# q placed by transfers, context loads four units ahead, ternary weights and expert loads moved, in a two-pass cross-attention kernel

## The reference

```
def bit_quant(W):
    gamma = jnp.mean(jnp.abs(W))
    Wq = jnp.clip(jnp.round(W / (gamma + Q_EPS)), -1.0, 1.0) * gamma
    return W + jax.lax.stop_gradient(Wq - W)
...
q = xn @ bit_quant(Wq).T + bq
k = context @ bit_quant(Wk).T + bk
v = context @ bit_quant(Wv).T + bv
scores = jnp.einsum('bqhd,bkhd->bhqk', q, k) * SCALE
probs = jax.nn.softmax(scores, axis=-1)
out = jnp.einsum('bhqk,bkhd->bqhd', probs, v).reshape(B, T, C)
return residual + (out @ bit_quant(Wo).T + bo)
```

## Time and profile before

| | |
|---|---|
| median of 3 runs | 638.69 us (638.66 to 639.59) |
| the profiled execution | 638.79 us, its span 637.0 us |
| mean granted clock of TensorE | 0.935 of full |
| TensorE busy | 544.5 us (85% of the span) |
| VectorE busy | 425.6 us (67%) |
| ScalarE busy | 326.7 us (51%) |
| GpSimd busy | 152.7 us (24%) |
| windows of the first pass | 106 to 327 us |
| windows of the second pass | 431 to 627 us |

### The profile page before, as it was taken

How to read it: one execution, slowest core, us unless ns; L and a number is a source line. 1 busy time by engine, 2 the same in 40 slices (tenths; PEclk the granted TensorE clock), 3 DMA queues, 4 the chain that set the end, 5 groups by cost and what they waited for, 6 DMA issues and landing times.

```text
span 637.0 us, 16158 instructions
## 1 busy us (share of the span) xinstructions
PE 544.5 (85%) x6582; PEld 383.9 (60%) x6582; DVE 425.6 (67%) x1090; ACT 326.7 (51%) x495; POOL 152.7 (24%) x128
## 2 busy tenths in 40 slices
PE   0699838589999999999967989468999999999996
PEld 0587515266766667676745767234666767667674
DVE  5667478679998999977224302569787687786730
ACT  0165214356666576765743333215566567676573
POOL 1554212313241524300015100223041240421000
PEclk9899668889999999999997989878999999999998
DMA  5010733434436353342200642026536436353300
GB/s 154 32 50 1 164 92 69 126 88 110 132 74 172 72 139 75 75 99 50 100 1 1 170 108 66 9 84 146 137 80 175 121 77 168 88 137 75 74 3 15
DMA packets 25338, 57.44 MB, mean 90 GB/s; under 512 B 4660, under 2 KB 8876, under 8 KB 25268
## 3 DMA queue, kind: packets, MB, share of 16 engines
q1 hardware_dynamic: 25268, 56.45, 34.6%
HBM read 17.81 MB, written 0.23 MB: 28 GB/s over the span
## 4 chain that ended last, share of the span: by engine, by line
PE 45%; DVE 23%; issue 21%; DMA 4%; POOL 3%; ACT 2%; SPq 2%; DVEq 0%; POOLq 0%; ACTq 0%
DVE mxp L791 11%; PE SM L1170 10%; PE PO L1185 9%; PE ST L1149 6%; PE MI L1101 6%; DMA cx<-in_ctx 3%; PE MI L1091 3%; DVE cx L779 3%; DVE qst L815 2%; PE MI L1125 2%; PE SM L1257 2%; DVE ksplit L786 1%; DVE cstat L763 1%; PE SM L1125 1%; DVE xn L732 1%
## 5 line engine op out<-in xcount | busy, mean ns | idle before, releaser
L791 DVE TENSOR_REDUCE mxp<-SM 112x1 f32<-112x500 f32 x364 | 235.2, 673 | 60.5 <-PE SM L1170 59.1
L593 ACT ACTIVATE PT<-ST 128x896 f32<-128x896 f32 x192 | 171.1, 911 | 49.7 <-PE ST L1149 49.1
L1170 PE MATMUL SM<-kst,qst 96*112 96x500 bf16 x364 | 143.1, 407 | 24.7 <-DVE mxp L791 24.1
L1149 PEld LDWEIGHTS ST<-qst,kst 98*128 98x128 bf16 x1536 | 95.0, 100 | 32.6 <-issue 9.7
L1149 PE MATMUL ST<-qst,kst 98*128 98x112 bf16 x1536 | 108.5, 215 | 1.2 <-DMA qst<-mrow 1.2
L471 POOL TENSOR_TENSOR kr<-kf,ksplit 128x500 f32<-128x500 f32 x48 | 56.1, 1170 | 184.4 <-ACT ksplit L565 184.3
L1185 PE MATMUL PO<-PT,vaug 125*32 125x112 f32 x3072 | 96.5, 264 | 2.1 <-ACT PT L593 1.5
L1170 PEld LDWEIGHTS SM<-kst,qst 96*112 96x112 bf16 x364 | 46.8, 131 | 66.9 <-DVE mxp L791 55.2
L1185 PEld LDWEIGHTS PO<-PT,vaug 125*32 125x32 f32 x3072 | 70.5, 110 | 24.5 <-issue 14.9
L577 ACT ACTIVATE vaug<-MI 125x512 f32<-125x512 f32 x48 | 28.7, 598 | 79.4 <-PE MI L1101 79.4
L476 POOL TENSOR_TENSOR ksplit<-kr,ksplit 128x500 bf16<-128x500 f32 x48 | 54.5, 1135 | 53.4 <-DVE ksplit L786 53.4
(11 more groups left out here) (129 smaller groups left out, 555.4 us busy)
## 6 DMA issues: line engine op xcount, KB each, us to landing
kst<-ksplit SPq DMA_DIRECT2D x192, 187.5 KB, 3.8
cx<-in_ctx SPq DMA_DIRECT2D x8, 750.0 KB
xT<-in_ctxT SPq DMA_DIRECT2D x8, 750.0 KB, 4.6
moe<-in_w1T SPq DMA_DIRECT2D x8, 256.0 KB, 2.9
moe<-in_w2T SPq DMA_DIRECT2D x8, 256.0 KB, 3.3
qall<-qsplit SPq DMA_DIRECT2D x12, 112.0 KB, 2.3
watt<-in_watt SPq DMA_DIRECT2D x1, 768.0 KB, 5.8
qst<-mrow SPq DMA_DIRECT2D x32, 1.8 KB
```

What stands on the lines that cost most here:

```text
L593: nc.scalar.activation(PT[:, k % PTB], ST[:, k % 2, :, 0:4 * PC], ACT.Exp, scale=SCALE).then_inc(exp_done, 1)
L791: nc.vector.tensor_reduce(mxp[:, j // 3, j % 3:j % 3 + 1], tile_bank(j, banks), AX.X, ALU.max).then_inc(sm_red, 1)
L1149: last = mm(ST[:, k % 2, cc, PC * p:PC * (p + 1)], kst[n.par][:, 4 * half + p, at:at + 128], qst[n.par][:, 4 * half + p], start=True, stop ...
L1170: mm(tile_bank(j, banks), qst[n.par][0:SROWS, j // 3], kst[n.par][0:SROWS, j // 3, at:at + THIRD], start=True, stop=True).then_inc(sm_full, 1)
```

## The change

1. `place_q` stays for the first unit of each pass. For all others a new function `place` on SyncE copies q into `qst` by two transfers per half (one per head of the pair), each 48 rows by 4 pairs by 56 elements of bf16. The zeros come from a memset of GpSimd at the start. TensorE waits for the transfers by a new function `q_here`.
2. In the first pass `load_ctx` is issued for n+4 where it was for n+3; the load of u3 moves to behind `load_qall(0)`.
3. The ternary weights move from behind `split_q(0)` into the window of u5, behind the maxima of step 6.
4. The loads of the first two experts move to the ends of SyncE's windows 3 and 4.

```
+            def place(n, half):
+                if n.c == 1:
+                    sp.wait_ge(qall_loaded, 16 * TERMS * (n.s + 1))
+                if n.s or n.c >= 2:
+                    sp.wait_ge(st_full, (n + -2).count(STEPS, HSTEP * (half + 1)))
+                pairs = slice(4 * half, 4 * half + 4)
+                for hh in range(2):
+                    rows_of = slice(hh * DH * TERMS, (hh + 1) * DH * TERMS)
+                    sp.dma_start(qst[n.par][rows_of, pairs, L * hh:L * (hh + 1)],
+                                 qall[rows_of, pairs, L * n.c:L * (n.c + 1)]).then_inc(q_placed[half][n.par], 16)
...
             def window(n):
-                if n.s == 0 and (n + 3).exists():
-                    load_ctx(n + 3)
+                if n.s == 0 and (n + 4).exists():
+                    load_ctx(n + 4)
                 if (n + 1).exists():
+                    place(n + 1, 1)
                     restack(n + 1, 1)
                 shift(n, 1)
                 if (n + 2).exists():
+                    place(n + 2, 0)
                     restack(n + 2, 0)
                 if (n + 1).exists():
                     shift(n + 1, 0)
                 if n.s == 1 and (n + 3).exists():
                     load_xT(n + 3)
+                if n.s == 0 and n.c in (3, 4):
+                    load_expert(n.c - 3, n.c - 3)
...
-            load_expert(0, 0)
-            load_expert(1, 1)
             load_qall(0)
+            load_ctx(Unit(0, None, 3))
             shift(u0, 0)
+            place(u1, 0)
             restack(u1, 0)
             run_windows(0, window)
...
             shift(v0, 0)
+            place(v0 + 1, 0)
             restack(v0 + 1, 0)
...
             for s in range(2):
+                nc.gpsimd.memset(qst[s][0:SROWS], 0.0)
                 last = nc.gpsimd.memset(kst[s][0:SROWS, :, T:TPAD], 0.0)
...
-                        if k == Q2_STEP:
-                            place_q(nxt, 1)
-                        if k == Q1_STEP and k_unit.exists():
-                            place_q(k_unit, 0)
...
+                    if n.s == 0 and n.c == B - 3 and k == HSTEP:
+                        ternary_weights()
...
-                    if j == START_TILES - 2:
-                        place_q(first + 1, 0)
...
+            def q_here(n, half):
+                if n.c == 0:
+                    pe.wait_ge(qst_ready, 2 * n.s + half + 1)
+                else:
+                    pe.wait_ge(q_placed[half][n.par], 32 * (n.s * (3 + n.par) + n.c // 2 + n.par))
```

More of the change, by code:

```diff
@@ L303, in build_kernel @@
             sem("mparts_ready"), sem("mx_full"), sem("mx_evac"))
+        q_placed = [[sem(f"q_placed{h}{p}") for p in range(2)] for h in range(2)]
         shift_loaded = [[sem(f"shift_loaded{h}{p}") for p in range(2)] for h in range(2)]
@@ L810, in place_q @@
                     dve.wait_ge(ld_member, 32)
-                if n.s or n.it is not None or n.c >= 2:
+                if n.s:
                     dve.wait_ge(st_full, (n + -2).count(STEPS, HSTEP * (half + 1)))
@@ L836, in add_projection, with ternary_weights @@
                                         ).then_inc(x_added, 1)
+            def ternary_weights():
+                dve.wait_ge(gam_ready, 1)
+                nc.vector.tensor_scalar(thr[:, 0], gam[:], EPS, 0.5, ALU.add, ALU.mult)
+                nc.vector.tensor_scalar(thr[:, 1], gam[:], EPS, -0.5, ALU.add, ALU.mult).then_inc(thr_ready, 1)
+                dve.wait_ge(thr_ready, 1)
+                for w in range(4):
+                    nc.vector.tensor_scalar(wt[:, 0, w], watt[:, 2, w], thr[:, 0, w:w + 1], None, ALU.is_gt)
+                    last = nc.vector.tensor_scalar(wt[:, 1, w], watt[:, 2, w], thr[:, 1, w:w + 1], None, ALU.is_lt)
+                last.then_inc(tern1, 1)
+                dve.wait_ge(tern1, 1)
+                nc.vector.tensor_tensor(wt[:, 0], wt[:, 0], wt[:, 1], ALU.subtract).then_inc(tern2, 1)
+                dve.wait_ge(tern2, 1)
+                for w in range(4):
+                    last = nc.vector.scalar_tensor_tensor(out=wt[:, 1, w], in0=wt[:, 0, w], scalar=gam[:, w:w + 1],
+                                                          in1=watt[:, 2, w], op0=ALU.mult, op1=ALU.subtract)
+                last.then_inc(tern3, 1)
+                dve.wait_ge(tern3, 1)
+                nc.vector.tensor_tensor(watt[:, 2], watt[:, 2], wt[:, 1], ALU.add).then_inc(wq_ready, 1)
             def window(n):
@@ L932, in _ @@
             split_q(0)
[L935 to L951, removed]
             def start_pass(s):
@@ L1158, in scores @@
                     output_forth(n + -1)
+            def q_here(n, half):
[3 more added lines that the diff above has]
+                    pe.wait_ge(q_placed[half][n.par], 32 * (n.s * (3 + n.par) + n.c // 2 + n.par))
             def max_tile(n, j, banks=2):
                 if j == 0:
-                    pe.wait_ge(qst_ready, n.count(2, 1))
+                    q_here(n, 0)
                     pe.wait_ge(kst_loaded[0][n.par], n.par_count(16 * TERMS, 16 * TERMS))
                 if j == TILES // 2:
-                    pe.wait_ge(qst_ready, n.count(2, 2))
+                    q_here(n, 1)
                     pe.wait_ge(kst_loaded[1][n.par], n.par_count(16 * TERMS, 16 * TERMS))
```

## The result

The changed kernel took 635.05 us (median of 19 runs, 630.94 to 639.86), the kernel before 641.01 in the runs beside it (19 runs, 638.25 to 645.78): a ratio of 0.992 [0.990, 0.994]. That is 6.0 us less by the medians and 5.2 by the ratio. The profiled execution took 634.5 us, its span 632.6, against 638.8 and 637.0. The forecast was 631, with a range of 625 to 637; the measured time lies inside the range.

The account below looks back on a forecast made before the run. TensorE and VectorE were both taken as nearly full in first-pass windows, TensorE alone in the second. The terms summed to -7.6 us from 638.8, giving 631 us, range 625 to 637.

Parts of the forecast that it names:

- The stall of u0's window: u0's window: u3's context load issued earlier ends TensorE's idling and low clock, -8.8 us, 0.9 taken back for the queue: -7.9.
- The setup: Start of first pass: ternary weights out gives 0.55 us, two placement issues delay u1's keys; between -0.5 and +1.0, taken +0.3.
- VectorE's placements: Windows of u1 to u4: sparing VectorE its placements gives 0.8 us each, bounds nothing to 1.4; -3.2 us in all.
- The price of small runs: Placement transfers: 384 runs of 112 bytes per half at 48 ns each, 1.15 us per half, ahead of the keys.
- u5's window: Ternary weights hold VectorE and delay step 8's tile +4.2 us; lower clock behind the gap +2.5; spared placements -0.5.
- The second pass: Windows of v1 to v6: placements off VectorE give 0.5 us each, bounds 0 and 0.75; -3.0 us in all.
- v0: Second pass's first unit: keys issued 1.3 us later, behind placements, so v1's first tile comes later; +0.7 us.
- VectorE's time is worth something: Denies the rival that VectorE's time is worth nothing in full windows: 638.6 us, no change, chance 0.10.
- The windows don't give all they hold: Denies the rival that windows gain their full bounds, 1.4 us and 0.75 each: at best 626 us, chance 0.10.
- The clock did fall in u5's window: Denies the rival that the clock does not fall in u5's window: 628.5 us, chance 0.17.
- The stall did move into the queue: Rival: load ahead of keys and maxima row costs 2 us in u0's window, 1 in each of u1 to u3; 635, chance 0.14.
- The slower rival: Placement transfers: 112-byte runs cost three times 48 ns, delaying keys in four windows, +9.2 us; about 642, chance 0.09.

Follow-up runs that it names:

- e3: The changed kernel with the context load three units ahead again, as before the change; 640.48 us, ratio 0.999 to the kernel before.
- e4: The kernel before with only the context loads moved four units ahead; 633.12 us, ratio 0.989.
- e2: The changed kernel with q placed by VectorE again as before, all else as changed; 638.65 us, ratio 0.997 to the kernel before.
- e6: The changed kernel with the ternary weights moved into u7's window; 627.47 us, ratio 0.982 to the kernel before.
- e8: The changed kernel with each placement's runs cut into four of 28 bytes; 634.4 us, ratio 0.990 to the kernel before.
- e5: The changed kernel with the n+4 context load issued behind the second-half placement, keys and maxima row; 632.04 us, ratio 0.988 to the kernel before.
- e7: The changed kernel with ternary weights in u7's window, context load behind keys and maxima row, each pass's first placement ahead of the maxima row; 627.94 us, ratio 0.981.
- e9: The kernel of e7 with the second pass's xT load issued ahead of the next unit's maxima row; 625.75 us, ratio 0.974 to the kernel before.
- e1: The changed kernel with the ternary weights back behind split_q(0) in the setup; 628.64 us, ratio 0.980 to the kernel before.

## Why the prediction was right, and where it was off

**The stall of u0's window** (-7.9): from u1's first tile to step 6 it was 19.40 us and is 11.46, which is -7.9, and e3 and e4 show that the load's distance alone makes it. The same places, in us behind the first score of u0's window:

| kernel | q placed by | u1's first tile | step 6 | step 3 of u1 |
|---|---|---|---|---|
| before | VectorE | 7.40 | 26.80 | 50.62 |
| e4 | VectorE | 6.43 | 18.69 | 42.53 |
| e2 | VectorE | 6.64 | 18.68 | 42.37 |
| change | transfers | 7.91 | 19.37 | 42.43 |
| e6, e8 | transfers | 7.95, 7.85 | 19.14, 19.33 | 42.17, 42.36 |
| e5 (load behind) | transfers | 7.94 | 18.68 | 41.75 |
| e7, e9 (also placed early) | transfers | 6.67, 6.60 | 18.16, 19.63 | 41.23, 42.72 |

Of the 2 us that late transfers might have cost there, e5 finds about 0.5 at step 6. In e1 and e8 TensorE waits 0.3 and 0.45 us for the maxima row there. The prediction worked out from the Trainium skill that the whole 2 us would be paid; the traces show a quarter of it. e9, with the same code as e7 in this pass, is 1.5 us slower at step 3; its clock was at the lower level twice in this window, as in the change's profile, in e7 once. One sign failed: the prediction named "a clock of 1.00 there", and behind u1's first tile the clock is at its lower level for 3.41 us in the change and in every other kernel with the early load. In e4 no wait of TensorE ahead of it was longer than 1.1 us. Before the change it was 10.2 us, so the larger part came back. Of the other signs, L815 (now L835) has its 8 instructions and the windows of the second pass are near 25.0; those of u1 to u3 are not near 27.2, for which see below.

**The setup** (+0.3): the keys came 0.9 later, the tile 0.1; e1 confirms that the ternary weights had been hidden there but for 0.6 us. The first column of the table shows the price of the two issues ahead of the keys more plainly: 1.3 us, taken back by the early placement of e7. TensorE waits 1.36 us for those keys in the change's profile and 2.4 to 2.5 in e1, e5, e6 and e8. The setup itself takes up to 2.6 us more or less between executions of the same code, so that the agreement of the first stretch within 0.7 us is luck in part: e8 ends it at 149.80, the change at 148.08.

**VectorE's placements** (-3.2 for u1 to u4): the size was right, e5's four windows are 3.65 us shorter than before, 0.9 each where 0.8 was taken. The step that failed is "0 to 1.1 us late in the windows of u1 to u3; I take 0": the lateness was 1.07, 0.52 and 0.52. The estimate of when the keys would land was right; the lower bound was the wrong end to pick. In e4 the bound of 0 did hold, with no placements ahead of the keys. The rule on engines in the Trainium skill (DMA: Bandwidth & Descriptors, Why a DMA increments its semaphore by 16 and not by 1) speaks for the upper bound: by it a load of 125 rows runs on the five lowest-numbered engines. The landings agree as far as they go (6.4 us behind the load, 1.9 without), but no row names the engines, so that the load and the transfers behind it share them stays a reading. That the load's place in the order makes the loss is shown by e5. In e9 a load delays the maxima row behind it in the same way.

**The price of small runs** (1.15 us per half) was four times too high; it entered only v0's term and the lateness above, so little came of it. The Trainium skill (the same page, Specifications) says that below 512 bytes an engine reads, modifies and writes. Whether that adds to the price of a run, no run here can tell: e8 made the same packets as the change. The prediction's sum for four times the row's price also has a slip: 3.45 us more per half in four windows give 645, not 644, which changes nothing.

**u5's window** (+4.2 and +2.5, less 0.5): the gap was 4.12, the low clock lasted 3.4 us, which costs 1.7, at the lower end of the range (1.75); the block in all costs 5.5. In all four other kernels with the block there (e2, e3, e5, e8) the gap was 4.12 too, but the low clock lasted twice as long, 3.4 us lost, and the window took 29.0 to 29.7. So 2.5 lies between the two; only one of five executions lost as little as 1.7, and that the change's profile is that one is luck. The clock didn't fall there in any kernel without the block (before, e1, e4, e6, e7, e9).

**The second pass** (-3.0 for v1 to v6): 0.62 in each of the four full windows, as e2 shows, 0.35 in v5's and nothing in v6's; the late load of `xT` took 0.4 back. The forecast had no term for it: SyncE's order was followed up to the keys and the maxima row, and not to what is issued last. **v0** (+0.7): from the maxima row's issue to the tile 9.94 us against 9.19, so +0.75. **GpSimd's memsets and the expert loads** (nothing): no run moves them alone. Between the passes TensorE waits 3.1 us for expert weights in the change's profile, 2.2 before, and 1.6 to 2.4 in the other traces, so that nothing points to the moved loads.

**The end** (+1.8) had no term. The clock falls near the end of both kernels, at 633.1 before and at 624.7 after, and in the changed one it caught the last projections:

```profile
624.70:632.60 7.90, 4.20 (x13) 2.63 (x12) 0.69 (x1) 0.00 (x0) 0.00 (x0) 0.50 0.12 29
```

4.2 us of work at half speed, where the same instructions of before (from 633.1: 0.22) ran nearly all at full. The moment of the fall differs between executions, and with it the end, from 9.6 to 11.9 us over the eleven traces; so one pair of traces doesn't show this loss to be an effect of the change. It is part of the spread of several us that each kernel's runs have.

**The balance.** Of the 7.6 us of the forecast the profile shows 4.4. u0's and u5's stretches gave 1.7 more than their terms. The windows of u1 to u4 gave 1.7 less (late keys), the second pass 0.6 less (`xT`, mostly), u6 0.4 less, the stretch with v0 0.5 less and the end 1.8. The medians show 6.0: the profile of the change drew a long stretch between the passes and a long end. So the mechanisms of the large terms held, and that the total came within 4 us rests in part on errors that cancelled.

**The rivals.** VectorE's time is worth something: e2 gives back 0.62 to 0.71 a window. The windows don't give all they hold (0.9 of 1.4 where nothing is late). The clock did fall in u5's window. The stall did move into the queue in part: 0.5 + 2.1 of the 5 us that this rival priced (2 in u0's window, of which the forecast had 0.9, and 1 in each of u1 to u3). The slower rival fell with the price of small runs.

## What to carry to other kernels

When a load is taken out of the way of one wait, follow it through the queue in which it now stands: what is issued behind it, small transfers above all, pays for its length, and the cheapest place here was behind the last transfer that the current window still needs. A block of work that an engine did under cover is worth moving only into other cover; in the fullest window it cost its whole length and the clock's fall on top. Experiments that change one place in an issue order at a time tell such costs apart where the total (5 us of 640, with a spread of several) can't: compare like stretches between fixed instructions, not spans.

## What the runs showed of the hardware

- A transfer of 112-byte runs between two places of SBUF took 12.5 ns of an engine's time a packet, against 48 ns for the packets of about 800 bytes of `qall`.
- Behind the same gap of 4.12 us in u5's window the granted clock stayed at its lower level (1.2 GHz) for 3.41 us in the change and for 6.83 in four others (e2, e3, e5, e8).
- In e4 it fell to that level for 3.41 us at 118.9, though the only waits of TensorE from 112 to 118.9 were 0.59, 0.66 and 1.07 us.
- A placement of 21 KB issued behind a 750 KB load on the same queue landed after 6.4 us, without the load after 1.9 (change, e5).
- A maxima row of 1.8 KB, issued right behind such a load, took 4.75 us (e9); one with no load just ahead took 1.69 (change, 103.92).
